# Layer 3's self attention: the mixing matmuls moved between the two scores of a pair

## What the reference computes there

```python
def _L3_attn_ref(x, proj_w, proj_b, wq, wk):
    ...
    H, hd = (NUM_HEADS, HEAD_DIM)
    proj = jnp.einsum('bsd,ed->bse', x, proj_w) + proj_b
    flat = jnp.transpose(proj.reshape(B, S, H, hd), (2, 0, 1, 3)).reshape(H, B * S, hd)
    q = jnp.einsum('hnd,hde->hne', flat, wq)
    k = jnp.einsum('hnd,hde->hne', flat, wk)
    logits = jnp.einsum('hne,hme->hnm', q, k) / jnp.sqrt(jnp.asarray(D, x.dtype))
    attn = jax.nn.softmax(logits, axis=-1)
    out = jnp.einsum('hnm,hmd->hnd', attn, flat)
    ...

x = x + _L3_attn_ref(_layernorm(x, axis=-1), L3_attn_proj_w, L3_attn_proj_b, L3_attn_wq, L3_attn_wk)
```

## Time and profile before

| | us |
|---|---|
| median of 3 runs | 3546.71 |
| the 3 runs | 3543.56 to 3554.42 |
| the profiled execution | 3540.32 |
| its span in the trace | 3538.3 |
| TensorE busy in the span | 3093.0 (87%) |
| phase "heads" in the trace (first products to last read-out) | 2473.5 to 3254.5 |

### The profile page before, as it was taken

How to read it: one execution, slowest core, us unless ns; L and a number is a source line. 1 busy time by engine, 2 the same in 40 slices (tenths; PEclk the granted TensorE clock), 3 DMA queues, 4 the chain that set the end, 5 groups by cost and what they waited for, 6 DMA issues and landing times. The chain is left out here.

```text
span 3538.3 us, 54754 instructions
## 1 busy us (share of the span) xinstructions
PE 3093.0 (87%) x18729; PEld 1841.2 (52%) x18729; DVE 2192.0 (62%) x4481; ACT 1752.6 (50%) x4108; POOL 1072.8 (30%) x1252
## 2 busy tenths in 40 slices
PE   5979739999888899988899989796899999998989
PEld 3656528877665556644455556363333333333656
DVE  5767645454556566677666565334888888884750
ACT  4958713333223244445556544112577777776531
POOL 2535644432432022224366631102111111111300
PEclk9989859999998899999999999797799999999999
DMA  9200145665530000031000041225011111101100
GB/s 330 86 9 1 41 176 189 208 196 168 161 97 25 25 1 1 1 104 72 38 1 1 1 172 44 107 75 167 9 19 19 19 19 19 19 1 50 49 5 20
DMA packets 155827, 242.91 MB, mean 69 GB/s; under 512 B 21027, under 2 KB 128180, under 8 KB 150100
## 3 DMA queue, kind: packets, MB, share of 16 engines
q1 hardware_dynamic: 141732, 201.64, 18.7%
q0 software_dynamic: 13824, 37.77, 3.3%
HBM read 132.23 MB, written 107.10 MB: 68 GB/s over the span
## 5 line engine op out<-in xcount | busy, mean ns | idle before, releaser
L4536 DVE TENSOR_REDUCE peaks<-ps 128x2 f32<-128x1024 f32 x512 | 604.4, 1219 | 135.5 <-PE ps L4485 134.2
L4573 ACT ACTIVATE attn<-ps 128x512 f32<-128x512 f32 x1024 | 529.0, 603 | 173.1 <-PE ps L4475 170.2
L4475 PE MATMUL ps<-queries,keys 50*128 50x512 f32 x1024 | 332.2, 427 | 56.0 <-ACT attn L4573 55.2
L4498 PE MATMUL ps<-attn,head_values 128*32 128x512 f32 x2048 | 274.9, 610 | 0.0
L4485 PE MATMUL ps<-keys,queries 50*128 50x512 f32 x1024 | 238.0, 462 | 12.7 <-DVE peaks L4536 8.1
L1196 POOL TENSOR_TENSOR attn_w<-attn_w,attn_share 128x512 f32<-128x512 f32 x128 | 131.7, 1050 | 375.5 <-DVE attn_share L1042 375.5
L4475 PEld LDWEIGHTS ps<-queries,keys 50*128 50x128 f32 x1024 | 144.4, 188 | 188.4 <-ACT attn L4573 171.2
L2084 PE MATMUL ps<-experts,tileT 128*128 x884 | 233.2, 386 | 2.8 <-issue 2.8
L2285 DVE COPY normed<-ps 128x256 f32<-128x256 f32 x221 | 93.7, 424 | 205.2 <-PE ps L2100 109.8
L4485 PEld LDWEIGHTS ps<-keys,queries 50*128 50x128 f32 x1024 | 98.3, 189 | 222.7 <-issue 185.6
L2100 PE MATMUL ps<-experts,hiddenT 128*128 (+1 forms) x474 | 146.7, 391 | 21.1 <-DVE hiddenT L2294 15.5
(11 more groups left out here) (703 smaller groups left out, 6993.2 us busy)
## 6 DMA issues: line engine op xcount, KB each, us to landing
tile_in<-routed_rows SPq DMA_DIRECT2D x244, 128.0 KB, 2.2
expert_rows<-normed SPq DMA_DIRECT2D x221, 128.0 KB
routed_rows<-zeros SPq DMA_DIRECT2D x2, 8064.0 KB, 45.1
experts<-in_L_ffn_experts SPq DMA_DIRECT2D x4, 3072.0 KB
routed_rows<-zeros SPq DMA_DIRECT2D x1, 12160.0 KB, 62.2
kT<-L_xattn_keys SPq DMA_DIRECT2D x8, 1024.0 KB
v<-L_xattn_values SPq DMA_DIRECT2D x8, 1024.0 KB, 7.5
experts<-in_L_ffn_experts SPq DMA_DIRECT2D x8, 1024.0 KB
```

The source lines that it names most:

```text
L4475: nc.tensor.matmul(bank(("score", n)), keys[pair % 2][rows, sl(kt)], queries[pair % 2][rows, sl(c, CHUNK)], start=True, stop=True).then_in ...
L4498: last = nc.tensor.matmul(mixed_bank[sl(strip, PAD), :], head_values[:, u // CHUNKS % 2, strip % 2, 2 * part + strip // 2, :], attn[:, (4 ...
L4536: v.tensor_reduce(peaks[:, r % 2, i // CHUNKS, :, i % CHUNKS], k.ps[:, at:at + 2, :], AX.X, ALU.max).then_inc(s["maxed"], 1)
L4573: nc.scalar.activation(attn[:, n % RING, :], bank(("score", n)), ACT.Exp, scale=1.0 / 16.0).then_inc(s["read"], 1)
```

## The change

One block in TensorE's list. Of a pair of scores, the second now waits until the mix has been issued, in every pair with n % 4 = 0; the mix no longer stands at the end of the step with n % 4 = 3. Which tiles are mixed is as before (`mix(n // 4 - 2)`), so at step 4k TensorE now mixes what it mixed at step 4k + 3. No other engine's list changes, and neither do banks, rings or the places of `out` and `unturn`.

```diff
                         for p in (n + LEAD, n + LEAD + 1):
                             if p < TOTAL:
                                 probe(p)
-                        for m in (n, n + 1):
-                            if scored(m):
-                                score(m)
-                    if n % 4 == 3 and scored(n - 8):
-                        mix(n // 4 - 2)
+                        if scored(n):
+                            score(n)
+                        if n % 4 == 0 and scored(n - 8):
+                            mix(n // 4 - 2)
+                        if scored(n + 1):
+                            score(n + 1)
                     if ended_at(n, UNTURN) is not None:
                         unturn(ended_at(n, UNTURN))
```

## The result

The changed kernel is slower: 3559.78 us median (3550.16 to 3565.23, 9 runs) beside 3541.85 (3536.34 to 3554.42, 9 runs), a ratio of 1.0046, interval 1.0031 to 1.0061. The forecast was 17 us faster, the measurement is 16 us slower by the ratio and 18 by the medians. The change is small, but its interval lies clear of 1. The profiled execution took 3554.62 us, its span is 3552.8.

What follows compares the result with a forecast made beforehand. A loop of waits through mix, probes, scores and exponential was taken to bound the kernel, 2.83 us a quad. Gaining 0.59 a unit over some 30 units, less 1.03 in the tail, gave -17: 3530 us, range 3519 to 3545.

Steps and rivals of the forecast that it cites:

- Step 1: Plain quads: score n + 3 no longer waits for the exponential of n; mixes 2.60 us apart against 2.83, 0.23 less.
- the tail: The last 12 quads, without probes: already at 2.60 us, they gain nothing and get one wait for the copy, +1.03.
- first rival: Probes take the gain back: VectorE gets its two probe pairs closer together, then nothing; 3537 to 3546 us, chance 15%.
- Step 2: The first mix of a unit newly waits for ScalarE's copy of the sum (`out`): loss of 1.03 us once a unit.
- Step 3: The quad with the transposes: they wait for the exponential of 13; 3.41 us against 3.42 today, so no gain.
- the sum: All units: 0.59 us gained in each, -17.6 over some 30 units; with the tail's +1.03, total -17, median 3530.
- The first units: First quads, at half clock: a mix sooner; together with the end put at -0.5 to +0.5 us.
- third rival: The clock falls: TensorE pauses over a microsecond before the mix in the copy's quad; slower, chance 6%.

## Why the prediction was wrong

- **Step 1 held.** A loop of waits sets the length of a quad, and no engine is busy all the time; 0.23 less in a plain quad was forecast, 0.22 to 0.23 came, by the chain named. The row of the tail that stood for it was the right one. One quad in a unit is 2.66 to 2.67, not 2.60. VectorE's transpose and reciprocal stand two to four us ahead of it (2847.21 and 2848.68, the quad is 2850.98 to 2853.64); whether they hold a probe there, as the first rival had it, was not followed up.
- **Step 2 held, 0.10 too small** (1.13 for 1.03), all of it between the copy's start and the mix (0.76 for 0.65). **Step 3 held, 0.08 too small** (3.49 for 3.41). With both, and with the quad of 2.67, 0.36 a unit is left instead of 0.59, so the sum without the clock is -11 and not -17.6 for the 30 units. The first units made up for some: they are 5.6 shorter, for which I had put 0.5 either way. Half clock ended 9 us sooner there, at 2514.6 instead of 2523.7, and a quad at half clock is 4.07 instead of 4.49. (The prediction says that half of what the quads gain goes to steps 2 and 3. By its own figures eight quads at 0.23 are 1.84 a unit, of which 0.59 is left, so it is two thirds; its sum doesn't use this.)
- **The clock failed.** The step that broke is the sum's assumption that the clock stays at 1.00 behind the pause of step 2: the sum put it at nothing, and the third rival, which had it, at 6%. That rival's mechanism and place were right: falls start at the mix behind the pause. A price of 1.9 for a fall of one quad, which is an estimate from the quad of 4.49 at half clock less 2.60, was near: 1.2 or 2.3 in one profile, 3.9 in the other. They came in eight units of 29 in the one and in every fourth in the other, not in every unit: 12.9 us of loss against the 10.5 that the order gains there. What misled me was the argument against it: "in the tail TensorE stands 0.45 in every 2.60 and the clock is 1.00 throughout". Pauses of 0.45 in each quad say nothing of one of 1.07, and one execution at 1.00 doesn't show a margin: in five of the six profiles with the new order and an unfilled end, the clock fell in just this tail. By the same estimate falls in a third of 31 units cost 31 / 3 x 1.9 = 20 us, more than the 17 of the forecast: that is nearly what happened.
- **The tail** was given +1.03 for its one wait, and cost 16.6 from the 241st mix on in the profile. No step had the clock falling there. How much of this the other executions paid isn't shown: filling the end made no difference to be seen in the ratio in three comparisons (0.9962 and 0.9963, 0.9876 and 0.9870, 0.9849 and 0.9837), each pair on different chips.
- Filling both places gives nearly the change that was forecast, -14 us, and filling the pause alone the same. So the failure is the clock's, and nothing else of size hides behind it. Taking the wait away gives -39, and -52 with the transposes moved too.

**Open.** Why the end falls in five of six profiles of the new order, and in that of the old order with the late copy, but not in those of before, of the old order filled and of the mix behind both scores, when all run a chain of 2.60 there, was not settled; the kernel with the transposes behind 13 did not fall either. Why the old order falls more under the same pause was not settled. Nor was why six falls remain when that pause is filled.

## What to carry to other kernels

Where a change brings a pause of a microsecond to a dense stream of matmuls (here 1.07 us, where TensorE was busy 556 of 600 us before), price what the clock does behind it, and don't take a granted clock of 1.00 before as proof of a margin: look at it first in the trace after. If falls are there, take the wait away (here by a place in another engine's list), and to test the cause put throw-away matmuls into the pause. And when a ring of banks makes a loop, count what stands between the big step and the one product that the next round waits for, not where the step stands in the list (2.61 us a quad with the mix between the two scores, 2.83 with it behind both).

## What the hardware showed that I had not expected

- A pause of 1.07 us in TensorE, in a stretch where it is busy more than 90% of the time, was enough for the granted clock to go from 1.00 to 0.50 behind it in some of the units (8 of 29 and 7 of 29), for 3.4 to 10 us in the changed kernel and up to 44 in the old order with the late copy. With half a microsecond less of pause (0.58) no fall came in 658 us. The sum of idle time isn't what tells the two kernels apart: it was larger in a unit of before (1.71 us), which never fell, than after (1.47).
- Adding matmuls made the kernel faster (1.0046 to 0.9962).
- Matmuls in the upper and lower 64 rows run beside each other also when the upper is issued first: they start at 2872.28 and 2872.29, and that of the upper rows is recorded as 0.49 long.
- TensorE's busy share went up (556 to 563 of 600 us) as the kernel got slower. Most of that is the new order, which has less idle time: between falls it is busy 71.52 of 76 us, or 94%, where before had 93%. In the falls it is 98 to 100% (9.81 and 10.00 of 10 us). So a busy share has to be read with the granted clock beside it.
